# Where the spare PSUM bank is used inside an attention slot: next-batch work ahead of the query product

## The chip, the cores and the metric

The kernel runs on one core of one Trainium2 chip. The metric is the device time of one execution in microseconds (us), lower is better. One core has a matmul engine (TensorE, PE in the rows, its weight loads PEld), VectorE (DVE), ScalarE (ACT), GpSimd (POOL) and a queue for transfers (SyncE, SP). They run side by side, each strictly in its own program order, and meet only at semaphores.

## What is computed

A transformer-like stack on x of 4 batches x 512 tokens x 256 features, all in float32: a latent attention (16 heads, query rank 192, key/value rank 64), a feed-forward block with looked-up weights, a state-space scan block and the feed-forward block again, each behind a layer norm and added to x. The change touches only the attention, cut here to what matters:

```python
q_c  = rms_norm(x @ wq_down.T, q_norm_w)           # rank 192
kv_c = rms_norm(x @ wkv_down.T, kv_norm_w)         # rank 64
q_nope, q_pe = heads(q_c @ wq_up.T), rope(heads(q_c @ wq_rope.T))
k_nope, v = split(heads(kv_c @ wkv_up.T));  k_rope = rope(x @ wk_rope.T)
scores = (q_nope . k_nope + q_pe . k_rope) / sqrt(192), causal
out = softmax(scores) @ v;  return out @ wo.T
```

## The kernel before

**Precision.** Every float32 product is made of reduced-precision passes: an operand is split into a high part (ScalarE rounds it, `..._hi`) and a low part (VectorE subtracts, `..._lo`), and TensorE makes three products. So each operand that TensorE makes for itself goes PSUM bank, ScalarE copy, VectorE subtraction, in that order.

**Units and slots.** The attention of a batch is 16 units: 4 query tiles of 128 tokens x 4 groups of 4 heads. Tile i attends to i + 1 key tiles. The units run in a software pipeline written out by hand, one slot per unit: in slot s TensorE makes the query product of unit s (`q_up`, L1496 to L1500, bank 0), transposes the queries of unit s-2 (`q_transpose`, L1507, bank 1), makes the scores of units s-2 and s-3 (L629 to L631, banks 2 and 3), transposes the probabilities of unit s-4 (`p_transpose`, L1533, banks 4 and 5), multiplies them with the values for unit s-5 (L1547, L1550, bank 6) and projects unit s-6 (L1560, L1562, bank 7). Each engine has its own slot function (`pe_slot`, `act_slot`, `dve_slot`) that fixes the order of its instructions, and slots of one batch run on into the next. Below, slots are numbered through from 0 to 63 (batch times 16, plus the unit whose query product lies in it).

**VectorE's order.** Between two `qt_low` (L1153, the low part of the transposed queries) it does in this order: row maxima of the third head (L1129, `row_max`), `pt_low` of key tile 0 (L1181), row maxima of the fourth head, `out_low` (L1187), then the reciprocals, further splits, row maxima of the first two heads, the rotation of the next queries (`rope_q`, L1143 to L1148), and the next `qt_low`. The row maxima wait for the scores of the same head.

**The spare bank.** Bank 1 holds the transposed queries for a part of a slot. In the rest of it, in 27 of the slots, it makes one piece of the next batch's input: in slots 4 to 7 of a batch a down product (`down`, six matmuls of 320 columns on L629 to L631; ScalarE copies it, `down_copy`, L792), in slots 9 and 10 the transposed normalised input of the batch after (`pe_xt_part`, four transposes on L594; `act_xt_part` L599, `dve_xt_part` L603), in slots 12 to 14 the transposes to feature-major form (`to_features`, four transposes on L1481; `feature_high` L813, `feature_low` L1121). In the last batch only slots 14 and 15 have such a piece, the input transposes for the feed-forward block. The counts are 12 down products, 4 pieces of input transposes, 9 of features and 2 at the end. Called here a spare piece.

**What guards the bank.** Before a spare piece TensorE waits until `qt_low` of unit s-2 has read the bank (`pe.wait_ge(qt_lo_s, 1 + b * UNITS + s - 1)`). Before the next `q_transpose` it waits until the spare piece has been read (`dp_cp`, `xt_lo_s` or `at_lo`). Both are waits of an engine that works in order: everything written behind them waits too.

**GpSimd** builds the feed-forward weights all the while, one tensor operation after the other, to about 490 us.

Of the kernel before, what the change touches and what calls it, by code (L numbers as in the profile page):

```python
# [12 lines left out]
BATCH, SEQ, DIM = 4, 512, 256  # L13
# [94 lines left out]
def build(nc, x_in, wq_down, wq_up, wq_rope, q_norm_w, wkv_down, kv_norm_w, wkv_up, wk_rope, wo,  # L108
# [3 lines left out]
    with ctx:  # L112
# [658 lines left out]
        def _(act):  # L771
# [90 lines left out]
            def act_slot(s, b, nb):  # L862
                def do(step, n, *k):
                    step_of(b, nb, step, n, *k)

                do(normalise, s - 4, 2)
                do(normalise, s - 4, 3)
                do(exp, s - 3, 0)
                do(pt_high, s - 5, 3)
                do(qt_high, s - 2)  # L870
                do(exp, s - 3, 1)
                do(pt_high, s - 4, 0)
                do(out_high, s - 5)
                u, m = ahead(s, b, nb)
                if 5 <= u <= 8 and m < BATCH:
                    mean_squares(m, u - 5)
                do(exp, s - 3, 2)
                do(pt_high, s - 4, 1)
                do(exp, s - 3, 3)
                do(q_copy, s)  # L880
                u, m = ahead(s, b, nb)
                do(normalise, s - 3, 0)
                if m == BATCH:
                    if u in (14, 15):
                        act_xt_part(m, u - 14, bank[1])
                else:
                    if 4 <= u <= 7:
                        down_copy(m, u - 4)
                    if u in (9, 10) and m + 1 < BATCH:
                        act_xt_part(m + 1, u - 9, bank[1])  # L890
                    if 12 <= u <= 14:
                        feature_high(m, u - 12)
                do(normalise, s - 3, 1)
                do(pt_high, s - 4, 2)
                if u in (10, 11) and m < BATCH:
                    query_scale(m, u - 10)
# [168 lines left out]
        def _(dve):  # L1065
# [130 lines left out]
            def dve_slot(s, b, nb, early=(0, 0)):  # L1196
# [20 lines left out]
                if s >= 2:  # L1217
                    dve_tasks(dve, *early)
                do(recip, s - 3, 0)
                between(0)  # L1220
                do(pt_low, s - 4, 1)
                between(1)
# [2 lines left out]
                do(recip, s - 3, 1)  # L1225
                between(3)
                do(row_max, s - 2, 0)
                if m == BATCH:
                    if u in (14, 15):
                        dve_xt_part(m, u - 14, bank[1])  # L1230
                else:
                    if u in (9, 10) and m + 1 < BATCH:
                        dve_xt_part(m + 1, u - 9, bank[1])
                    if 12 <= u <= 14:
                        feature_low(m, u - 12)
                between(4)
                do(normalise, s - 3, 2)
                between(5)
# [224 lines left out]
        def _(pe):  # L1463
# [102 lines left out]
            def pe_slot(s, b, nb):  # L1566
                def do(step, n, *k):
                    step_of(b, nb, step, n, *k)

                do(values, s - 5, 0)  # L1570
                do(p_transpose, s - 5, 3)
                do(scores, s - 3, 1)
                do(values, s - 5, 1)
                u, m = ahead(s, b, nb)
                if m == BATCH:
                    if u in (15, 16):
                        pe.wait_ge(xt_lo_s, 2 * m + u - 14)
                else:
                    if 5 <= u <= 8:
                        pe.wait_ge(dp_cp, m * TB + u - 4)  # L1580
                    if u in (10, 11) and m + 1 < BATCH:
                        pe.wait_ge(xt_lo_s, 2 * (m + 1) + u - 9)
                    if 13 <= u <= 15:
                        pe.wait_ge(at_lo, 3 * m + u - 12)
                do(q_transpose, s - 2)
                do(p_transpose, s - 4, 0)
                do(values, s - 5, 2)
                do(scores, s - 3, 2)
                do(values, s - 5, 3)
                do(q_up, s)  # L1590
                do(scores, s - 3, 3)
                do(p_transpose, s - 4, 1)
                if m == BATCH:
                    if u in (14, 15):
                        pe.wait_ge(qt_lo_s, 1 + b * UNITS + s - 1)
                        pe_xt_part(m, u - 14, bank[1])
                else:
                    if 4 <= u <= 7 or u in (9, 10) or 12 <= u <= 14:

                        pe.wait_ge(qt_lo_s, 1 + b * UNITS + s - 1)  # L1600
                    if 4 <= u <= 7:
                        if u == 4:
                            wait_xt(pe, m)
                        down(m, u - 4)
                    if u in (9, 10) and m + 1 < BATCH:
                        pe_xt_part(m + 1, u - 9, bank[1])
                    if 12 <= u <= 14:
                        if u == 12:
                            pe.wait_ge(tok_q, TB * m)
                            pe.wait_ge(tok, token_count(m, 12))  # L1610
                        to_features(m, u - 12)
                do(project, s - 6)
                do(p_transpose, s - 4, 2)
                do(scores, s - 2, 0)
# [195 lines left out]
```

## Time and profile before

| | |
|---|---|
| time, median of 3 runs | 825.81 us (823.83 to 827.28) |
| time of the profiled execution | 823.76 us |
| its span, first to last instruction | 821.8 us |
| mean granted TensorE clock | 0.988 |
| busy in the span | PE 91%, DVE 82%, ACT 74%, POOL 56% |
| attention slots, from query product 0 to the end of slot 63 | about 40 to 533 us |

The table is read from the page of the profiled execution. The 2 us between its time and its span lie before the first and behind the last instruction. A line such as "start, length, engine, line, op, out<-in" of the timeline is one instruction; brackets at its end hold how long the engine was idle before it and who ended that.

### The profile page before, as it was taken

What the parts mean: (1) busy time and instruction counts of PE and PEld (TensorE: products, weight loads), DVE (VectorE), ACT (ScalarE), POOL (GpSimd) and SP (SyncE); (2) the same over time, 40 slices, a digit from 0 to 9 for tenths busy, and PEclk for the clock granted to TensorE, in tenths of its full rate; (3) what the DMA queues carried; (4) which work ended last, traced back from release to release, by engine and by line L of the source; (5) the groups of instructions that cost most, each with busy time, mean ns of one, the idle gap of its engine ahead of it and who ended that gap; (6) DMA issues with size and microseconds to landing.
All of it is one profiled execution on the core that took longest, in us unless ns stands there. A gap on an engine that the chain in (4) does not pass through costs nothing.

```text
span 821.8 us, 15155 instructions
## 1 busy us (share of the span) xinstructions
PE 752.0 (91%) x4556; PEld 646.4 (79%) x4556; DVE 674.5 (82%) x2204; ACT 609.7 (74%) x1512; POOL 461.5 (56%) x388
## 2 busy tenths in 40 slices
PE   3775999999999999999999899999998999999998
PEld 3665887878877887888888788877887798887887
DVE  3667899999899999899999999996765878777643
ACT  2454999988999988899988899986537565674222
POOL 1599999999999999999999999400000000000000
PEclk9897999999999999999999999999999999999999
DMA  9800000000000000000000100000000000000000
GB/s 243 279 1 0 2 1 2 1 1 1 2 2 1 2 1 1 2 2 1 2 1 2 39 2 1 2 1 0 2 1 0 1 1 1 1 1 27 27 26 26
DMA packets 15376, 14.52 MB, mean 18 GB/s; under 512 B 5792, under 2 KB 14432, under 8 KB 15040
## 3 DMA queue, kind: packets, MB, share of 16 engines
q1 hardware_dynamic: 13792, 11.41, 4.7%
q0 software_dynamic: 624, 2.12, 0.8%
q8 instruction: 37, 0.61, 0.3%
q14 instruction: 43, 0.35, 0.1%
q10 hardware_dynamic: 880, 0.04, 0.1%
HBM read 11.46 MB, written 2.10 MB: 17 GB/s over the span
## 4 chain that ended last, share of the span: by engine, by line
PE 52%; ACT 18%; DVE 16%; issue 13%; DMA 1%; DVEq 0%; ACTq 0%; SPq 0%
PE bank L629 11%; PE bank L631 10%; PE bank L630 10%; ACT prob L840 5%; PE bank L1533 5%; ACT prob L820 4%; DVE pt_lo L1181 2%; ACT pt_hi L849 2%; PE bank L1550 2%; PE bank L1547 2%; PE bank L1560 1%; PE bank L1562 1%; DVE bias_m L1129 1%; PE bank L594 1%; DVE qt_lo L1153 1%
## 5 line engine op out<-in xcount | busy, mean ns | idle before, releaser
L760 POOL TENSOR_SCALAR hot<-raw_gu,lut 128x352 f32<-128x352 int32 x120 | 177.9, 1482 | 12.2
L766 POOL TENSOR_TENSOR total<-total,hot 128x352 f32<-128x352 f32 (+1 forms) x168 | 158.7, 945 | 14.0
L820 ACT ACTIVATE prob<-bank,bias_m 128x128 f32<-128x128 f32 (+3 forms) x256 | 136.5, 533 | 21.0 <-DVE bias_m L1129 20.5
L1129 DVE CUSTOM_DVE_ANT_0 bank<-bank,mask 128x128 f32<-128x128 f32 (+3 forms) x256 | 125.4, 493 | 19.1 <-issue 17.7
L1181 DVE TENSOR_TENSOR pt_lo<-bank,pt_hi 128x512 fp32r<-128x512 f32 x160 | 108.9, 681 | 8.6 <-ACT pt_hi L849 8.3
L1533 PE MATMUL bank<-ident,prob 128*128 128x128 f32 x640 | 99.1, 277 | 17.5 <-ACT prob L840 11.2
L840 ACT ACTIVATE prob<-prob,rden 128x128 f32<-128x128 f32 (+3 forms) x224 | 110.4, 545 | 4.9 <-DVE rden L1164 4.3
L849 ACT CAST pt_hi<-bank 128x512 fp32r<-128x512 f32 x160 | 94.2, 590 | 11.5 <-PE bank L1550 6.9
L1533 PEld LDWEIGHTS bank<-ident,prob 128*128 128x128 f32 x640 | 72.4, 140 | 36.7 <-ACT prob L840 20.2
L629 PE MATMUL bank<-kt_hi,qt_hi 128*128 128x128 f32 (+3 forms) x256 | 87.4, 341 | 4.3 <-ACT prob L820 2.0
L760 POOL TENSOR_SCALAR hot<-raw_dn,lut 128x352 f32<-128x352 int32 (+1 forms) x60 | 87.6, 1461 | 6.1
L630 PE MATMUL bank<-kt_lo,qt_hi 128*128 128x128 f32 (+3 forms) x256 | 82.8, 324 | 0.0
L631 PE MATMUL bank<-kt_hi,qt_lo 128*128 128x128 f32 (+3 forms) x256 | 82.8, 323 | 0.0
L629 PE MATMUL bank<-xt_hi,gu_hi 128*128 128x512 f32 (+1 forms) x176 | 70.1, 399 | 1.6 <-DVE h_f L1305 1.6
L1547 PE MATMUL bank<-pt_hi,v_hl 128*128 128x512 f32 x160 | 68.1, 426 | 3.1 <-issue 2.4
L631 PE MATMUL bank<-xt_hi,gu_lo 128*128 128x512 f32 (+1 forms) x176 | 69.4, 394 | 0.0
L630 PE MATMUL bank<-xt_lo,gu_hi 128*128 128x512 f32 (+1 forms) x176 | 69.3, 394 | 0.0
L1560 PE MATMUL bank<-wo_a,o_a 128*128 128x256 f32 x256 | 67.9, 298 | 0.1
L933 ACT ACTIVATE silu<-bank 128x512 f32<-128x512 f32 x40 | 24.0, 601 | 57.4 <-PE bank L631 57.4
L1550 PE MATMUL bank<-pt_lo,v_hl 128*128 128x512 f32 x160 | 63.5, 397 | 0.3 <-DVE pt_lo L1181 0.2
L1562 PE MATMUL bank<-wo_b,o_b 128*128 128x256 f32 x256 | 63.7, 282 | 0.0
L629 PEld LDWEIGHTS bank<-kt_hi,qt_hi 128*128 128x128 f32 x256 | 48.6, 190 | 14.6 <-ACT prob L820 3.1
(208 smaller groups left out, 2091.9 us busy)
## 6 DMA issues: line engine op xcount, KB each, us to landing
x<-in_L_attn_a_x_dram SPq DMA_DIRECT2D x4, 512.0 KB, 7.7
wo_nat<-in_L_attn_a_wo_dram SPq DMA_DIRECT2D x1, 2048.0 KB, 12.2
out_dram<-x SPq DMA_DIRECT2D x16, 128.0 KB, 1.8
wqu<-in_L_attn_a_wq_up_dram SPq DMA_DIRECT2D x2, 768.0 KB, 7.7
wqr<-in_L_attn_a_wq_rope_dram SPq DMA_DIRECT2D x4, 192.0 KB, 7.5
raw_dn<-in_L_ffn_down_idx_dram POOLq DMA_DIRECT2D x1, 688.0 KB, 11.0
raw_gu<-in_L_ffn_gate_idx_dram POOLq DMA_DIRECT2D x1, 640.0 KB, 7.5
raw_gu<-in_L_ffn_up_idx_dram POOLq DMA_DIRECT2D x1, 640.0 KB, 8.5
```

The source lines that it names most:

```text
L629: nc.tensor.matmul(o, l_hi, r_hi, start=start and k == 0, stop=False)
L630: nc.tensor.matmul(o, l_hi, r_lo, start=False, stop=False)
L631: last = nc.tensor.matmul(o, l_lo, r_hi, start=False, stop=stop and k == n - 1)
L760: nc.gpsimd.tensor_scalar((hot if v else total)[:, 0:n], raw[:, c:c + n], float(v), lut[:, v:v + 1], ALU.is_equal, ALU.mult).then_inc(lut_ ...
L766: nc.gpsimd.tensor_tensor(dst, total[:, 0:n], hot[:, 0:n], ALU.add).then_inc(lut_sum, 1)
L820: nc.scalar.activation(prob[:, n % 2, h, 0:w], bank[2 + h % 2][:, 0:w], ACT.Exp, bias=bias_m[:, n % 2, h:h + 1], scale=-1.0, accum_out=den ...
L840: nc.scalar.activation(prob[:, n % 2, h, 0:w], prob[:, n % 2, h, 0:w], ACT.Copy, scale=rden[:, n % 2, h:h + 1]).then_inc(norm_a, 1)
L849: nc.scalar.copy(pt_hi[:, c % 2, :, :].rearrange("p h d -> p (h d)"), bank[4 + c % 2][:, :])\
L1129: nc.vector.tensor_tensor_reduce(out=bank[2 + h % 2][:, 0:w], in0=bank[2 + h % 2][:, 0:w], in1=mask[:, TB * P - w:TB * P], scale=1.0, scal ...
L1181: nc.vector.tensor_tensor(pt_lo[:, c % 2, :, :].rearrange("p h d -> p (h d)"), bank[4 + c % 2][:, :], pt_hi[:, c % 2, :, :].rearrange("p h ...
L1533: last = nc.tensor.transpose(bank[4 + c % 2][:, h * P:(h + 1) * P], prob[:, n % 2, h, j * P:(j + 1) * P], ident[:, :])
L1547: nc.tensor.matmul(bank[6][:, :], v, pt_hi[:, c % 2, :, :].rearrange("p h d -> p (h d)"), start=j == 0, stop=False)
```

## The change

In each of the three slot functions the spare piece moves forward, and nothing is added or removed. On TensorE it stood behind `p_transpose(s - 4, 1)` and now stands ahead of `q_up(s)`; its wait for `qt_lo_s` moves with it. On ScalarE the copy of the piece moves ahead of `pt_high(s - 4, 1)`. On VectorE the subtraction moves from behind `row_max(s - 2, 0)` to behind `recip(s - 3, 0)`. The wait ahead of `q_transpose` stays.

```diff
--- before.py
+++ after.py
@@ -875,11 +875,6 @@
                 if 5 <= u <= 8 and m < BATCH:
                     mean_squares(m, u - 5)
                 do(exp, s - 3, 2)
-                do(pt_high, s - 4, 1)
-                do(exp, s - 3, 3)
-                do(q_copy, s)
-                u, m = ahead(s, b, nb)
-                do(normalise, s - 3, 0)
                 if m == BATCH:
                     if u in (14, 15):
                         act_xt_part(m, u - 14, bank[1])
@@ -890,6 +885,11 @@
                         act_xt_part(m + 1, u - 9, bank[1])
                     if 12 <= u <= 14:
                         feature_high(m, u - 12)
+                do(pt_high, s - 4, 1)
+                do(exp, s - 3, 3)
+                do(q_copy, s)
+                u, m = ahead(s, b, nb)
+                do(normalise, s - 3, 0)
                 do(normalise, s - 3, 1)
                 do(pt_high, s - 4, 2)
                 if u in (10, 11) and m < BATCH:
@@ -1217,6 +1217,14 @@
                 if s >= 2:
                     dve_tasks(dve, *early)
                 do(recip, s - 3, 0)
+                if m == BATCH:
+                    if u in (14, 15):
+                        dve_xt_part(m, u - 14, bank[1])
+                else:
+                    if u in (9, 10) and m + 1 < BATCH:
+                        dve_xt_part(m + 1, u - 9, bank[1])
+                    if 12 <= u <= 14:
+                        feature_low(m, u - 12)
                 between(0)
                 do(pt_low, s - 4, 1)
                 between(1)
@@ -1225,14 +1233,6 @@
                 do(recip, s - 3, 1)
                 between(3)
                 do(row_max, s - 2, 0)
-                if m == BATCH:
-                    if u in (14, 15):
-                        dve_xt_part(m, u - 14, bank[1])
-                else:
-                    if u in (9, 10) and m + 1 < BATCH:
-                        dve_xt_part(m + 1, u - 9, bank[1])
-                    if 12 <= u <= 14:
-                        feature_low(m, u - 12)
                 between(4)
                 do(normalise, s - 3, 2)
                 between(5)
@@ -1587,9 +1587,6 @@
                 do(values, s - 5, 2)
                 do(scores, s - 3, 2)
                 do(values, s - 5, 3)
-                do(q_up, s)
-                do(scores, s - 3, 3)
-                do(p_transpose, s - 4, 1)
                 if m == BATCH:
                     if u in (14, 15):
                         pe.wait_ge(qt_lo_s, 1 + b * UNITS + s - 1)
@@ -1609,6 +1606,9 @@
                             pe.wait_ge(tok_q, TB * m)
                             pe.wait_ge(tok, token_count(m, 12))
                         to_features(m, u - 12)
+                do(q_up, s)
+                do(scores, s - 3, 3)
+                do(p_transpose, s - 4, 1)
                 do(project, s - 6)
                 do(p_transpose, s - 4, 2)
                 do(scores, s - 2, 0)
```

On TensorE, slot 25 (a piece of input transposes, `xn`), before: the query product is `wa_hi` to `wb_lo` into a bank, `kt_hi`/`qt_hi` are scores, `prob` is the probability transpose.

```order
L1496 MATMUL bank<-wa_hi,qa_hi 128x512 [waits q_rope,qa_cp]
L1497 MATMUL bank<-wa_lo,qa_hi 128x512
L1498 MATMUL bank<-wa_hi,qa_lo 128x512
L1499 MATMUL bank<-wb_hi,qb_hl 128x512
L1500 MATMUL bank<-wb_lo,qb_hl 128x512
L629 MATMUL bank<-kt_hi,qt_hi 128x256 [waits s_exp]
L630 MATMUL bank<-kt_lo,qt_hi 128x256
L631 MATMUL bank<-kt_hi,qt_lo 128x256
L1533 MATMUL bank<-ident,prob 128x128 [waits pt_lo_s]
L1533 MATMUL bank<-ident,prob 128x128 x3
L594 MATMUL bank<-ident,xn 128x128 [waits xt_lo_s,ln_norm,qt_lo_s]
L594 MATMUL bank<-ident,xn 128x128 x3
```

and now:

```order
L594 MATMUL bank<-ident,xn 128x128 [waits xt_lo_s,ln_norm,qt_lo_s]
L594 MATMUL bank<-ident,xn 128x128 x3
L1496 MATMUL bank<-wa_hi,qa_hi 128x512 [waits q_rope,qa_cp]
L1497 MATMUL bank<-wa_lo,qa_hi 128x512
L1498 MATMUL bank<-wa_hi,qa_lo 128x512
L1499 MATMUL bank<-wb_hi,qb_hl 128x512
L1500 MATMUL bank<-wb_lo,qb_hl 128x512
L629 MATMUL bank<-kt_hi,qt_hi 128x256 [waits s_exp]
L630 MATMUL bank<-kt_lo,qt_hi 128x256
L631 MATMUL bank<-kt_hi,qt_lo 128x256
L1533 MATMUL bank<-ident,prob 128x128 [waits pt_lo_s]
L1533 MATMUL bank<-ident,prob 128x128 x3
```

The two `xn` rows with their wait for `qt_lo_s` went from the end of this stretch to its head; the query product, the scores of the fourth head and the probability transpose stand behind that wait.

On VectorE, the same slot, before: `o_b` is `out_low`, `rden` a reciprocal, `pt_lo` the low part of the probabilities, `rms_...` and `x` small steps of other work, `ISA bank,bias_m` the row maxima, `xt_lo` the subtraction of the spare piece.

```order
L1187 TENSOR_TENSOR o_b<-bank,o_a 64x512 [waits o_hi_s]
L1164 RECIPROCAL rden<-den 128x2 [waits norm_a,s_exp]
L529 SCALAR_TENSOR_TENSOR rms_r<-rms_t,rms_r 128x8 [waits rms_ref]
L1181 TENSOR_TENSOR pt_lo<-bank,pt_hi 128x512 [waits pv_mm,pt_hi_s]
L636 TENSOR_TENSOR x<-bank,x 128x256 [waits y_mm]
L525 TENSOR_TENSOR rms_t<-rms_r 128x8 [waits rms_ref]
L1164 RECIPROCAL rden<-den 128x2 [waits norm_a,s_exp]
L527 SCALAR_TENSOR_TENSOR rms_t<-rms_t,rms_v 128x8 [waits rms_ref]
L512 MEMSET scratch 128x1 [waits s_exp,s_mm]
L1129 ISA bank,bias_m<-bank,mask 128x256
L1129 ISA bias_m 128x1
L603 TENSOR_TENSOR xt_lo<-bank,xt_hi 128x512 [waits xt_hi_s]
```

and now:

```order
L1187 TENSOR_TENSOR o_b<-bank,o_a 64x512 [waits o_hi_s]
L1164 RECIPROCAL rden<-den 128x2 [waits norm_a,s_exp]
L603 TENSOR_TENSOR xt_lo<-bank,xt_hi 128x512 [waits xt_hi_s]
L529 SCALAR_TENSOR_TENSOR rms_r<-rms_t,rms_r 128x8 [waits rms_ref]
L1181 TENSOR_TENSOR pt_lo<-bank,pt_hi 128x512 [waits pv_mm,pt_hi_s]
L636 TENSOR_TENSOR x<-bank,x 128x256 [waits y_mm]
L525 TENSOR_TENSOR rms_t<-rms_r 128x8 [waits rms_ref]
L1164 RECIPROCAL rden<-den 128x2 [waits norm_a,s_exp]
L527 SCALAR_TENSOR_TENSOR rms_t<-rms_t,rms_v 128x8 [waits rms_ref]
L512 MEMSET scratch 128x1 [waits s_exp,s_mm]
```

`xt_lo` moved up by nine rows, past one `pt_lo`, one reciprocal and the row maxima of one head. It is still behind `o_b`, and so behind the row maxima of the fourth head, which stand ahead of `o_b`.

On ScalarE, the same slot, before: `prob,den` is the exponential of one head, `pt_hi` the high part of the probabilities, `q_tok` the copy of the query product.

```order
L820 ACTIVATE prob,den<-bank,bias_m 128x256 [waits s_max]
L849 CAST pt_hi<-bank 128x512 [waits pv_mm,pt_mm]
L820 ACTIVATE prob,den<-bank,bias_m 128x256 [waits s_max]
L827 COPY q_tok<-bank 128x4x64 [waits qt_mm,qa_mm]
L840 ACTIVATE prob<-prob,rden 128x256 [waits recip_s]
L599 CAST xt_hi<-bank 128x512 [waits xt_mm]
L840 ACTIVATE prob<-prob,rden 128x256 [waits recip_s] x3
```

and now:

```order
L820 ACTIVATE prob,den<-bank,bias_m 128x256 [waits s_max]
L599 CAST xt_hi<-bank 128x512 [waits xt_mm]
L849 CAST pt_hi<-bank 128x512 [waits pv_mm,pt_mm]
L820 ACTIVATE prob,den<-bank,bias_m 128x256 [waits s_max]
L827 COPY q_tok<-bank 128x4x64 [waits qt_mm,qa_mm]
L840 ACTIVATE prob<-prob,rden 128x256 [waits recip_s] x4
```

`xt_hi` moved ahead of `pt_hi`, of the last exponential, of the query copy and of one normalisation (`prob<-prob,rden`).

## Rows read from the trace of the kernel before

**Rows 1.** The page's section 2, busy tenths of the span in 40 slices.

```profile
...
PE   3775999999999999999999899999998999999998
...
DVE  3667899999899999899999999996765878777643
...
```

**Rows 2.** Windows: slots with down products, with xn, with features, and the last two.

```profile
...
sum 72.34, PE 68.92 PEld 62.02 DVE 61.83 ACT 67.73 POOL 67.29; mean PE 22.97 PEld 20.67 DVE 20.61 ACT 22.58 POOL 22.43
...
sum 30.53, PE 28.00 PEld 23.92 DVE 30.14 ACT 29.45 POOL 28.40; mean PE 14.00 PEld 11.96 DVE 15.07 ACT 14.72 POOL 14.20
...
sum 74.44, PE 72.60 PEld 63.26 DVE 68.55 ACT 72.34 POOL 69.15; mean PE 24.20 PEld 21.09 DVE 22.85 ACT 24.11 POOL 23.05
...
519.49:536.95 17.46, 16.85 (x101) 13.95 (x101) 15.95 (x53) 15.87 (x39) 3.73 (x4) 1.00 0.01 1
...
```

**Rows 3.** Waits over the span: engine, line, releaser: us in total, times, longest.

```profile
...
PE bank L1507 <- DVE xt_lo L603: 2.2, 4, 1.2
```

**Rows 4.** Timeline of slot 21, a down product: start us, length us, instruction.

```profile
...
209.45 0.45 PE L1496 MATMUL bank<-wa_hi,qa_hi 128*128 128x512 f32 x1
209.47 0.69 DVE L1153 TENSOR_TENSOR qt_lo<-bank,qt_hi 128x512 fp32r<-128x512 f32 x1
...
210.31 0.69 DVE L1181 TENSOR_TENSOR pt_lo<-bank,pt_hi 128x512 fp32r<-128x512 f32 x1
...
210.93 0.36 PE L629 MATMUL bank<-down_hi,xt_hi 128*128 128x320 f32 x1
...
211.14 0.29 DVE L1129 CUSTOM_DVE_ANT_0 bank<-bank,mask 128x128 f32<-128x128 f32 x1
...
211.86 0.28 PE L1560 MATMUL bank<-wo_a,o_a 128*128 128x256 f32 x1
...
213.89 0.63 PE L1507 MATMUL bank<-ident,q_tok 128*128 128x128 f32 x4
...
214.65 0.60 ACT L832 CAST qt_hi<-bank 128x512 fp32r<-128x512 f32 x1
...
215.27 0.47 PE L1496 MATMUL bank<-wa_hi,qa_hi 128*128 128x512 f32 x1
...
```

**Rows 5.** Timeline of slot 25, a piece of input transposes.

```profile
...
234.65 0.40 PE L1496 MATMUL bank<-wa_hi,qa_hi 128*128 128x512 f32 x1
...
235.00 0.68 DVE L1153 TENSOR_TENSOR qt_lo<-bank,qt_hi 128x512 fp32r<-128x512 f32 x1
...
235.95 0.68 DVE L1181 TENSOR_TENSOR pt_lo<-bank,pt_hi 128x512 fp32r<-128x512 f32 x1
236.05 0.28 PE L631 MATMUL bank<-kt_hi,qt_lo 128*128 128x256 f32 x1
...
236.60 0.60 PE L594 MATMUL bank<-ident,xn 128*128 128x128 f32 x4
...
236.96 0.36 PE L1560 MATMUL bank<-wo_a,o_a 128*128 128x256 f32 x1
...
240.25 0.68 DVE L603 TENSOR_TENSOR xt_lo<-bank,xt_hi 128x512 fp32r<-128x512 f32 x1
...
240.98 0.66 PE L1507 MATMUL bank<-ident,q_tok 128*128 128x128 f32 x4 [1.18 <-DVE xt_lo L603]
...
```

**Rows 6.** Timeline of slot 29, a piece of feature transposes.

```profile
...
266.51 0.68 DVE L1153 TENSOR_TENSOR qt_lo<-bank,qt_hi 128x512 fp32r<-128x512 f32 x1
...
266.73 0.39 PE L1496 MATMUL bank<-wa_hi,qa_hi 128*128 128x512 f32 x1
...
267.60 0.68 DVE L1181 TENSOR_TENSOR pt_lo<-bank,pt_hi 128x512 fp32r<-128x512 f32 x1
...
268.63 0.56 DVE L1129 CUSTOM_DVE_ANT_0 bank<-bank,mask 128x384 f32<-128x384 f32 x1 [0.35 <-issue]
...
```

**Rows 7.** L1148 (79 to 530 us; busy, mean ns, idle), then min/median/max ns.

```profile
...
L1148 DVE TENSOR_TENSOR q_tok<-q_tok,q_rot 128x256 f32<-128x256 f32 x59 | 34.4, 582 | 2.0
...
L1148 DVE TENSOR_TENSOR q_tok<-q_tok,q_rot x64: 424/426/1216, 43.8 to 535.9; 128x256 f32<-128x256 f32 x64
...
```

## The prediction

> **What bounds the kernel now.** I read the page first: from slice 5 to slice 27 TensorE and VectorE both stand at eight or nine tenths [rows 1]. There are two full engines, so a wait on either can cost, and the share of busy time does not say which. I then took the windows of the slots that hold a spare piece. Each window runs from the end of one `qt_low` to the end of a later one, so that it holds whole VectorE periods: 80.74 to 104.17, 204.07 to 228.53 and 329.38 to 353.83 us for the 12 down products, 111.27 to 126.07 and 235.67 to 251.40 for the 4 `xn` pieces, 134.20 to 158.91, 259.53 to 284.25 and 382.18 to 407.19 for the 9 feature pieces, and 519.49 to 536.95 for the last 2 [rows 2]. A sum row gives the length of the windows and each engine's busy time in them. Subtracting, VectorE is idle 72.34 - 61.83 = 10.51, 30.53 - 30.14 = 0.39, 74.44 - 68.55 = 5.89 and 17.46 - 15.95 = 1.51 us, 18.30 us in all 27 periods. TensorE is idle 3.42 + 2.53 + 1.84 + 0.61 = 8.40 us. Neither has more than a few tenths of a microsecond to give in a slot, save VectorE in the down slots, with 0.88 us each.
>
> **What the move takes away.** The wait it can remove is the one ahead of `q_transpose`, where TensorE waits for `xt_lo` to be read out of bank 1. That is 2.2 us in 4 waits [rows 3], 1.18 us of it in slot 25: `xt_lo` runs from 240.25 to 240.93 and the transposes start at 240.98 [rows 5]. A semaphore therefore costs 0.05 us from end to start; I use that below. On VectorE `xt_lo` now stands nine rows earlier, so this wait should go. For down products and features no such wait shows, so nothing goes there.
>
> **What the move adds.** TensorE's wait for `qt_lo_s` stood 210.93 - 209.45 = 1.48 us behind the start of `q_up` in slot 21 [rows 4], where `qt_low` was long over. Now it stands where `q_up` started. Read both: in slot 21 TensorE started `q_up` at 209.45 and `qt_low` ended at 209.47 + 0.69 = 210.16 [rows 4]; in slot 25 it was 234.65 against 235.68 [rows 5]; in slot 29, 266.73 against 267.19 [rows 6]. TensorE would idle 0.71, 1.03 and 0.46 us, plus 0.05 each. Taken as the price per slot this gives 12 x 0.76 + 4 x 1.08 + (9 + 2) x 0.51 = 19.1 us, less 2.2 removed: 16.9 us. That is the ledger of TensorE.
>
> It is not the whole price, because of what is queued behind that wait: the spare piece itself, `q_up`, the scores of the fourth head, a probability transpose. VectorE's row maxima of the fourth head wait for those scores, and behind these row maxima stand all of `out_low`, the reciprocals, the rotation and the next `qt_low`. In place of running beside `qt_low`, the query product now lies between it and these row maxima. The ledger of VectorE, slot by slot:
> - Down, slot 21 [rows 4]. The piece takes 211.86 - 210.93 = 0.93 us. The row maxima start 211.14 - 209.45 = 1.69 us behind the start of `q_up`. New start: 210.16 + 0.05 + 0.93 + 1.69 = 212.83. VectorE is ready when `pt_low` ends, 210.31 + 0.69 = 211.00. It waits 1.83 us.
> - `xn`, slot 25 [rows 5]. The piece takes 236.96 - 236.60 = 0.36 us, and the scores end 236.33 - 234.65 = 1.68 us behind `q_up`. New start: 235.68 + 0.05 + 0.36 + 1.68 + 0.05 = 237.82, ready at 236.63: 1.19 us.
> - Features, slot 29 [rows 6]. Four transposes too, taken at 0.36 us; the row maxima start 268.63 - 266.73 = 1.90 us behind `q_up`. New start: 267.19 + 0.05 + 0.36 + 1.90 = 269.50, ready at 268.28: 1.22 us. The last 2 slots are taken as these.
>
> New waits: 12 x 1.83 + 4 x 1.19 + 11 x 1.22 = 22.0 + 4.8 + 13.4 = 40.2 us. VectorE does no more work than before, so its old idle time in the same periods, 18.3 us, is used up first. That leaves 21.9 us. The removed wait on `xt_lo` is not subtracted again: in these slots VectorE was busy in 30.14 of 30.53 us [rows 2], so the time TensorE gains there is time in which VectorE still has to work.
>
> Between the two ledgers, 16.9 and 21.9, I take VectorE's. TensorE's lag is itself made by the lateness of VectorE, and a period of VectorE cannot be shorter than its work and its waits.
>
> **Does the loss build up or wash out?** From below: if VectorE and ScalarE caught up behind the first wait, the lag would shrink to the bare chain. In slot 21 the query transposes take 0.63 us, the ScalarE copy 0.60 and `qt_low` 0.69, with two semaphores 2.02 us, while TensorE has 215.27 - 213.89 = 1.38 us of other work until `q_up` [rows 4]. So 0.64 us stays in each down slot, whatever the others do: 7.7 us for the 12. For the other slots I take no floor, and part of the 2.2 us is given back; about 7 us in all. From above: if VectorE's old idle time were only half usable, because it lies behind other waits, the sum would be 40.2 - 9.2 = 31 us. I keep 7 and 31 as the ends.
>
> **ScalarE.** Its copy of the piece moves into a stretch in which it now waits: the transposes for `pt_hi` and the scores for the last exponential come later by the piece and the wait. The copy costs nothing there, and as much less follows later. ScalarE was busy in 67.73 of 72.34 us in the down slots [rows 2], so it has little to give; its stream shifts with VectorE's, and I add nothing. If it were the one that ends last, the loss would lean to the upper end.
>
> **One outside influence on the lag.** L1148, the last step of the rotation, stands right ahead of `qt_low`. It takes 424 ns at best, 582 in the mean and 1216 at most [rows 7]; its operands are the same each time.
>
> The Trainium skill, SBUF — State Buffer, "Practical consequences", says that a VectorE instruction with two inputs in SBUF contends with a GpSimd instruction that reads SBUF, and that the later one blocks until the first is done. L1148 has two such inputs and GpSimd runs at that time, which would explain the spread. By that rule slots of another length meet GpSimd at other phases: with every L1148 of the 27 slots at 424 ns the sum would fall by 27 x 0.16 = 4.3 us, and with all of them held as long as the longest it would rise by 27 x 0.63 = 17 us. Which phase the changed kernel falls into no row tells.
>
> I leave the mean of 582 ns in the sum, as the rows have it.
>
> **The sum.** 823.76 us, the profiled execution, plus 21.9 gives 845.7. The median of the runs shown is 2.05 us above the profiled execution. I forecast 846 us, about half way towards the lower ledger with that offset added (823.8 + 2.0 + 20.2).
>
> **The rivals.**
> 1. Mostly absorbed, slower by 7 to 13 us, 831 to 837. After the first wait of each series the engines behind catch up, and only the bare chain of the down slots is left. For it: VectorE has 0.88 us idle per down slot. Against it: in the `xn` slots it has none.
> 2. It builds up, 856: ScalarE or the waits behind the fourth head's scores push the next `qt_low` further than TensorE's own delay, so the upper end of 31 us is met. For it: TensorE and ScalarE are both above nine tenths in the down slots [rows 2].
> 3. The other side, faster, about 821: the new wait hides in the idle time that TensorE has anyway. TensorE idles 8.40 us in these slots [rows 2]. If `qt_low` came so much earlier that the new wait fell under 0.3 us per slot, it would fit in there (27 x 0.3 = 8.1), and 2.2 us of `xt_lo` waits and a little more would be the net gain. This is decided by the lag between `q_up` and the end of `qt_low`; it must fall from 0.46 to 1.03 us to under 0.3. Against it stands the bare chain in the down slots, 0.64 us.
> 4. No change, 824 to 826: that waits cancel gains. It needs the same collapse of the lag, a little less of it.
>
> That the change does not take effect is excluded: the rows of all three engines are in another order.
>
> **How the numbers follow.** The forecast, 838 to 852, has a chance of 0.70; rival 1 has 0.15, rival 2 0.08, rival 3 0.03, rival 4 0.04. What this measurement can tell from no change is about 0.5%, 4.1 us. The first three are all slower by more than that: 0.93. Faster 0.03, same 0.04. The range reaches from 832, in rival 1, to 857, which takes in the upper end with its offset.
>
> **What will show it.** Right: in slots with a spare piece, the first instruction of the piece (L629 with `down_hi`, L594, L1481) has an idle time of 0.5 to 1.2 us ahead of it, ended by VectorE's `qt_lo`, 27 times; VectorE waits 1.2 to 1.8 us for the fourth head's row maxima; the waits of L1507 on `xt_lo` are gone; the 12 down periods last about 72.3 + 22.0 - 10.5 = 84 us in place of 72.3, and the feed-forward part is unchanged. Wrong: if the waits ahead of the pieces add up to under 8 us, `qt_low` does not lag as I read it; if they are there and the span has grown by much less, TensorE had slack that its busy share hides; if slots without a piece have grown, another engine carries the delay on.

## The result and the profile after

The changed kernel takes 865.62 us (857.65 to 867.28, 4 runs), against 826.54 us before on the same chip: ratio 1.047, 95% interval 1.044 to 1.051. The forecast was 846, slower by 20 us; it came out slower by 39. The direction and the place were right, the size was off by nearly a factor of two, and the time lies outside the stated range.

The page after, section 2: busy tenths per fortieth of the span, here 864.5 us, and the granted clock.

```profile
...
PE   4756778999888899888899999999998999999998
...
DVE  3676697899688889768889899898766778787643
...
PEclk9797999999899999999999999999999999999999
...
```

In the attention slots TensorE and VectorE have fallen together, in many slices from nine tenths [rows 1] to eight or less. Where the time went shows in the windows of the same 27 VectorE periods, found again by the ends of the same `qt_low`. First the three series of down products: stretch, length, busy time of PE, PEld, DVE, ACT, POOL, then the granted clock.

```profile
...
81.27:112.27 31.00, 25.55 (x152) 22.02 (x153) 20.33 (x90) 23.43 (x83) 28.88 (x24) 0.95 0.00 1
220.19:254.50 34.31, 29.36 (x168) 25.32 (x169) 22.46 (x94) 23.27 (x83) 31.91 (x27) 0.90 0.00 1
359.24:391.15 31.91, 26.42 (x169) 22.82 (x170) 21.48 (x90) 23.35 (x83) 29.67 (x25) 1.00 0.01 2
sum 97.22, PE 81.33 PEld 70.16 DVE 64.27 ACT 70.04 POOL 90.46; mean PE 27.11 PEld 23.39 DVE 21.42 ACT 23.35 POOL 30.15
```

Then the sums of the `xn` slots (2 windows) and of the feature slots (3 windows), and the window of the last two.

```profile
...
sum 38.29, PE 32.80 PEld 27.91 DVE 31.15 ACT 30.14 POOL 35.61; mean PE 16.40 PEld 13.96 DVE 15.57 ACT 15.07 POOL 17.81
...
sum 82.16, PE 76.43 PEld 66.11 DVE 68.08 ACT 72.56 POOL 76.31; mean PE 25.48 PEld 22.04 DVE 22.69 ACT 24.19 POOL 25.43
...
559.13:578.27 19.14, 18.35 (x106) 15.15 (x107) 16.04 (x53) 16.46 (x40) 0.00 (x0) 1.00 0.01 1
...
```

Against [rows 2] the periods grew by 24.9, 7.8, 7.7 and 1.7 us, 42.0 of the span's 42.7 us. So nearly the whole growth of the profiled execution lies in the periods with a piece. Who waited for whom on TensorE: the line that waited, the releaser, us in total, times, longest.

```profile
...
PE bank L629 <- DVE qt_lo L1153: 15.0, 12, 2.0
PE bank L1533 <- ACT prob L840: 13.5, 35, 0.9
PE bank L1481 <- DVE qt_lo L1153: 6.4, 9, 1.3
PE bank L594 <- DVE qt_lo L1153: 5.4, 6, 1.4
...
PE bank L1496 <- DVE qt_lo L1153: 1.7, 2, 1.1
...
```

The guard on `qt_low` costs TensorE 28.5 us in 29 waits. The wait for `xt_lo` [rows 3] is gone, as the change meant. Two of the 29 waits stand at L1496, the query product itself. In slots 41 and 42, in the third batch, the guard is executed though no piece follows: `u in (9, 10)` brings the guard, and only the piece asks for `m + 1 < BATCH`. I had counted pieces, not guards.

One down slot, 38, at full clock: start, length, engine, line, operation; brackets give the idle time before and its end.

```profile
...
372.61 0.63 PE L1507 MATMUL bank<-ident,q_tok 128*128 128x128 f32 x4
...
373.47 0.57 ACT L832 CAST qt_hi<-bank 128x512 fp32r<-128x512 f32 x1
...
373.89 1.03 DVE L1148 TENSOR_TENSOR q_tok<-q_tok,q_rot 128x256 f32<-128x256 f32 x1
...
374.84 0.68 DVE L1153 TENSOR_TENSOR qt_lo<-bank,qt_hi 128x512 fp32r<-128x512 f32 x1
...
375.57 0.41 PE L629 MATMUL bank<-down_hi,xt_hi 128*128 128x320 f32 x1 [1.36 <-DVE qt_lo L1153]
...
376.56 0.39 PE L1496 MATMUL bank<-wa_hi,qa_hi 128*128 128x512 f32 x1
...
378.21 0.29 DVE L1129 CUSTOM_DVE_ANT_0 bank<-bank,mask 128x128 f32<-128x128 f32 x1 [1.86 <-issue]
...
378.60 0.37 ACT L820 ACTIVATE prob<-bank,bias_m 128x128 f32<-128x128 f32 x1 [1.38 <-DVE bias_m L1129]
...
```

Read it downwards: query transposes, then the copy, over at 373.47 + 0.57 = 374.04 us; `qt_low` starts 0.80 us later, held back by a long L1148; TensorE is released 0.05 us behind its end; the piece, the query product, and at 378.21 the row maxima of the fourth head, for which VectorE waited 1.86 us (the forecast had 1.83). ScalarE's exponential then waits 1.38 us for those. In slot 21 before, TensorE and VectorE did not wait there [rows 4], and neither did ScalarE.

This slot is no exception in what held `qt_low` back. VectorE's row for it over the whole span: count, busy us, mean ns, idle us before it.

```profile
...
L1153 DVE TENSOR_TENSOR qt_lo<-bank,qt_hi 128x512 fp32r<-128x512 f32 x64 | 43.7, 683 | 0.6 <-ACT qt_hi L832 0.2
...
```

VectorE was idle only 0.6 us in total ahead of all 64, 0.2 us of it for the copy. In the timeline, the 27 `qt_low` that a piece waits for start on average 0.65 us behind the end of their copy (0.57 before the change); in 25 of them the copy had been over for 0.27 us or more, and what ended last was VectorE's own work ahead of it: the last step of the rotation (L1148) in 19 of the 27, small steps for the next batch in most others.

### The profile page after: what moved, and what is told of

Same layout as the page of the kernel before. It is cut to its first block, busy times and chain, and to the rows that moved or that the text cites. A ratio compares the mean times of both kernels' runs of the same rounds, so it can differ in the third digit from the quotient of the medians.

```text
span 864.5 us, 15154 instructions
## 1 busy us (share of the span) xinstructions
PE 764.8 (88%) x4556; PEld 654.0 (76%) x4556; DVE 675.6 (78%) x2204; ACT 611.8 (71%) x1512; POOL 460.7 (53%) x388
## 4 chain that ended last, share of the span: by engine, by line
PE 50%; DVE 21%; issue 18%; ACT 9%; DMA 1%; DVEq 0%; ACTq 0%; SPq 0%
PE bank L629 10%; PE bank L631 10%; PE bank L630 10%; PE bank L1533 4%; DVE pt_lo L1181 3%; ACT prob L840 3%; ACT prob L820 2%; DVE qt_lo L1153 2%; DVE bias_m L1129 2%; DVE o_b L1187 2%; PE bank L1550 2%; PE bank L1547 2%; ACT pt_hi L849 2%; PE bank L594 2%; PE bank L1560 1%
## 5 line engine op out<-in xcount | busy, mean ns | idle before, releaser
L1129 DVE CUSTOM_DVE_ANT_0 bank<-bank,mask 128x128 f32<-128x128 f32 (+3 forms) x256 | 125.7, 495 | 60.3 <-issue 57.2
L766 POOL TENSOR_TENSOR total<-total,hot 128x352 f32<-128x352 f32 (+1 forms) x168 | 158.2, 942 | 14.0
L1533 PE MATMUL bank<-ident,prob 128*128 128x128 f32 x640 | 99.3, 278 | 19.1 <-ACT prob L840 13.5
L840 ACT ACTIVATE prob<-prob,rden 128x128 f32<-128x128 f32 (+3 forms) x224 | 107.1, 541 | 5.8 <-DVE rden L1164 5.1
```

The source lines that it names most:

```text
L766: nc.gpsimd.tensor_tensor(dst, total[:, 0:n], hot[:, 0:n], ALU.add).then_inc(lut_sum, 1)
L840: nc.scalar.activation(prob[:, n % 2, h, 0:w], prob[:, n % 2, h, 0:w], ACT.Copy, scale=rden[:, n % 2, h:h + 1]).then_inc(norm_a, 1)
L1129: nc.vector.tensor_tensor_reduce(out=bank[2 + h % 2][:, 0:w], in0=bank[2 + h % 2][:, 0:w], in1=mask[:, TB * P - w:TB * P], scale=1.0, scal ...
L1533: last = nc.tensor.transpose(bank[4 + c % 2][:, h * P:(h + 1) * P], prob[:, n % 2, h, j * P:(j + 1) * P], ident[:, :])
```

## The experiments

Each time below stands beside the kernel before on the same chip, 825.3 to 826.3 us. Ratios are to it, with the 95% interval. The edits are shortened: `(guard, piece)` stands for the wait on `qt_lo_s` and the spare piece behind it.

**Which pieces?** `down_early`: only the down products moved, on TensorE and ScalarE. `others_early`: all but them moved.

```diff
+if down_slot:  (guard, down)      # others_early: if not down_slot
 do(q_up, s)
 do(scores, s - 3, 3)
 do(p_transpose, s - 4, 1)
+if not down_slot:  (guard, piece)
```

> Only the 12 down products stand ahead of the query product (TensorE) and ahead of the probability split (ScalarE); the xn, feature and last pieces stay where they were before. Theory A (each moved piece puts the wait for qt_low ahead of the query product, and the row maxima of the fourth head wait for it; the prices of the kinds of piece simply add): the down periods grew by 23.9 us in the trace of the changed kernel, so about 848 to 852 us here, clock below 0.985. Rival B (the pieces spoil each other, the delay of one series is carried into the next by ScalarE): clearly less than its share, under 840 us.

> The 15 other pieces (xn, features, the last two) stand early on all three engines, the down products as before; the guard on qt_low stands early in every slot that had it. Theory A: 6.2 + 8.0 + 1.4 us of their periods plus 1.8 us of two slots that have the guard and no piece, 17 us, so about 842 to 845 us. The early guard ahead of the query product also stands in the two slots of batch 3 without a piece. Rival B: under its share, near 835 us, with the missing rest appearing only when both moves are made together.

Measured: 847.79 us, 1.025 (1.021 to 1.030), and 843.56 us, 1.022 (1.019 to 1.024). The added times over the kernel before, some 21 and 18 us (2.53% and 2.16% of 826), add up to 39, with some 4 us of uncertainty, and both moves together gave 39.1. Theory A stands: each moved piece has its own price, and B, that one series spoils the next, is refuted to within that.

**The guard or the piece?** `guard_only` is the kernel before with the guard alone ahead of `q_up`. `behind_q_up` has piece and guard between `q_up` and the scores of the fourth head, so late that the guard hardly waits. `guard_all` is `guard_only` with the guard in all 60 slots from slot 4 on.

```diff
 # guard_only                                   # behind_q_up
+if slot_has_guard:                              do(q_up, s)
+    pe.wait_ge(qt_lo_s, 1 + b*UNITS + s - 1)   +(guard, piece)
 do(q_up, s)                                     do(scores, s - 3, 3)
```

> The kernel before, with only the guard added: in the slots that have one, TensorE also waits for qt_low ahead of the query product; the pieces themselves and ScalarE and VectorE stay where they were. Theory A (VectorE's wait for the fourth head's row maxima sets the price, and of its old idle time only that at the same place is used up): 0.58 x 12 + 0.83 x 4 + 0.33 x 11 + 1.8 us, about 16 us, and some 3 us for the clock: 840 to 846 us. Rival F (only the wait of TensorE counts and the piece ahead of the query product costs nothing): the whole loss appears here, 860 us or more.

> ScalarE and VectorE as in the changed kernel, on TensorE the piece and its guard directly behind the query product and ahead of the scores of the fourth head. qt_low is over by then (the lag is under the 1.2 us of a query product in all but a few slots), so what is left is that the scores, and the row maxima behind them, come later by the piece. Theory A: 0.93 x 12 + 0.36 x 15, less 2.2 us of waits for xt_lo, about 14 us and no more falls of the clock: 836 to 842 us. Rival F: about 824 to 828 us, since no wait of TensorE is added.

> The kernel before with the guard on qt_low ahead of the query product in all 60 slots from slot 4 on, in place of the 29 of guard_only: the suspected cost doubled. Theory A (each guard costs about 0.83 us, since qt_low lags by that in every slot): 826 + 60 x 0.83 = 876 us, 870 to 885. Rival K (the cost is one of changing from one rhythm to another, and washes out where the wait is everywhere): under 860 us.

Measured: `guard_only` 850.46 us, 1.030 (1.026 to 1.034); `behind_q_up` 834.37 us, 1.010 (1.008 to 1.011); `guard_all` 884.24 us (2 runs), 1.071 (1.069 to 1.073). TensorE's waits in the first and in the last, and the one left in `behind_q_up` on a down product:

```profile
...
PE bank L1496 <- DVE qt_lo L1153: 26.6, 29, 1.7
...
```

```profile
...
PE bank L1496 <- DVE qt_lo L1153: 53.8, 60, 2.0
...
```

```profile
...
PE bank L629 <- DVE qt_lo L1153: 1.1, 1, 1.1
...
```

The guard alone costs 24.2 us for 26.6 us of waiting, and 60 guards cost 58.9 for 53.8. In these two kernels what TensorE waits there is lost nearly one for one, and K, that the cost washes out where the wait is everywhere, is refuted. My theory A had 14 to 20 us for `guard_only`, by VectorE's ledger, and was short again; rival F, that the guard is everything, was too high. The piece ahead of the scores costs 8.1 us by itself, under the 10 to 16 I expected; F, which had it at nothing, fails here as well. Together 32.3 of 39.1 us. That the two prices simply add is assumed, not shown.

**Whose lateness makes the lag?** Four kernels cut one VectorE instruction to 32 of its 512 columns, `out_low` (not between the transposes and the guard) or `qt_low` (between them), in the changed kernel and in the one before.

```diff
+if b or n > 1:      # changed_light, before_light: out_low; changed_qt_light, before_qt_light: qt_low
+    nc.vector.tensor_tensor(<32 columns>, ..., ALU.subtract).then_inc(<the same semaphore>, 1)
+    return
```

> The changed kernel with out_low (L1187) cut from 512 to 32 columns in all but the first two units: it leaves out most of the low part of the attention output, so only its time is read. out_low stands directly behind the row maxima of the fourth head on VectorE and takes some 0.6 us per slot. Theory H (the ring wait for qt_low, query product, row maxima, VectorE's stream, next qt_low sets the period of a slot with a piece): the time falls by about 0.5 us x 29 slots more than in the kernel before with the same cut: by 15 us or more, to 846 to 852 us. Rival J (the ring goes over the query transposes and ScalarE's copy): it falls by no more than the kernel before does.

> The kernel before with the same cut of out_low, the control of changed_light; most of the low part of the attention output is left out. VectorE is the fullest in the xn slots and in the slots of the fourth query tile, so some of the 0.6 us x 64 is seen there: 812 to 822 us under either theory. What counts is the difference to the changed kernel's fall.

> The changed kernel with qt_low (L1153) cut from 512 to 32 columns in all but the first two units: it leaves out most of the low part of the transposed queries, so only its time is read. VectorE loses the same 0.6 us per slot as in changed_light, but here the cut lies between the query transposes and the guard. Theory J (the price is TensorE's wait for the chain query transposes, ScalarE's copy, qt_low, whatever else VectorE has to do): the waits ahead of the pieces fall from 29 us by about 0.5 us each, and the time by at least 14 us, to 851 us or less, clearly more than the 6 us that the cut of out_low gave. Theory H (VectorE's whole stream sets the period): the same 6 us as there, 859 us.

> The kernel before with the same cut of qt_low, the control. Nothing waits for qt_low itself here before the scores 2 us later, so what is seen is VectorE's relief alone: about as with the cut of out_low, 815 us, 810 to 820, under either theory.

| cut | before, us and ratio | changed, us and ratio | fall of before | fall of changed |
|---|---|---|---|---|
| none | 826.54, 1 | 865.62, 1.0471 | | |
| `out_low` | 814.85, 0.9869 | 859.34, 1.0415 | 0.0131, 10.8 us | 0.0056, 4.6 us |
| `qt_low` | 822.54, 0.9954 | 848.75, 1.0261 | 0.0046, 3.8 us | 0.0210, 17.3 us |

The falls are differences of the ratios, times 826 us; each ratio has an interval of 0.002 to 0.004 to either side, so the falls of the changed kernel are good to some 4 us. Either cut takes 0.50 us off each of 62 instructions (684 to 184 ns, 683 to 181). The same relief of VectorE is worth 12.7 us more in the changed kernel when it is taken from `qt_low` itself, and less than half as much in the kernel before, where I had expected 810 to 820 us and was wrong. The waits of the down products and of the feature pieces in `changed_light`, then in `changed_qt_light`. The inserted lines move L1481 to L1485, and in the second L1153 to L1154:

```profile
...
PE bank L629 <- DVE qt_lo L1153: 15.8, 12, 2.0
...
PE bank L1485 <- DVE qt_lo L1153: 4.7, 9, 0.9
...
```

```profile
...
PE bank L629 <- DVE qt_lo L1154: 6.1, 10, 1.5
...
PE bank L1485 <- DVE qt_lo L1154: 2.5, 5, 0.8
...
```

H's forecast failed and J's came true: `out_low`, though it stands in VectorE's stream to the next `qt_low`, gives little, and the 29 waits stay as they are (28.4 us in `changed_light`, 28.5 without the cut); `qt_low` itself gives 17.3 us, 0.6 per guard. That the length of `qt_low` is part of the price is thus shown. J as a whole is not: it names the query transposes and ScalarE's copy as what comes before, and in the changed kernel the copy was over 0.65 us ahead of `qt_low`. Part of what `out_low` gave up turned into waiting further on in VectorE's order; its idle time ahead of the row maxima, 60.3 us in the changed kernel, is here

```profile
...
L1129 DVE CUSTOM_DVE_ANT_0 bank<-bank,mask 128x128 f32<-128x128 f32 (+3 forms) x256 | 125.7, 495 | 69.5 <-issue 64.6
...
```

No run cut the row maxima or the rotation, which stand between.

**Bringing `qt_low` forward.** In the slots ahead of a piece, `qt_low` moves ahead of the rotation.

```diff
+if next_slot_has_piece: do(qt_low, s - 1)
 do(rope_q, s)
 ...
-do(qt_low, s - 1)
+if not next_slot_has_piece: do(qt_low, s - 1)
```

> The changed kernel, but in the slots ahead of a piece VectorE makes qt_low ahead of the rotation of the next queries, so that the rotation (1.3 us) fills VectorE's wait for the fourth head's row maxima and qt_low is over sooner. Theory A: the row maxima's wait falls from 2.2 to about 0.9 us in a down slot, and what is left is the bare chain transposes, copy, qt_low: 838 to 846 us. Rival G (ScalarE's or TensorE's own stream carries the loss, VectorE's order is second to it): 856 us or more.

Measured 865.71 us, 1.045 (1.039 to 1.050): nothing gained. My expectation of 838 to 846 failed, and the time is in the range of rival G. A wait of VectorE, then three of TensorE (the query product is L1502 here, the feature transposes L1487):

```profile
...
DVE qt_lo L1153 <- ACT qt_hi L832: 20.5, 27, 1.2
...
```

```profile
...
PE bank L629 <- DVE qt_lo L1153: 7.4, 10, 2.2
PE bank L1487 <- DVE cd L1110: 7.4, 3, 2.8
PE bank L1502 <- DVE q_rot L1146: 5.7, 17, 1.4
...
```

The guards did come free sooner: TensorE waits for `qt_low` 9.7 us in all (7.4 at down products, 2.3 at `xn` pieces) in place of 28.5. But `qt_low` now stands waiting for the copy for 20.5 us, with the rotation behind it. The next query product waits until the rotation has read its bank, 5.7 us in place of 0.5, and three feature pieces wait 7.4 us for L1110, the last step of the next batch's key rotation, which stood ahead of `qt_low` and now stands behind it. So 18.8 us less waiting at the guard bought no time: the one-for-one rule of `guard_only` holds for a guard moved along TensorE's order, not for every way of shortening its wait. The profiled execution is also the slowest of the four, at a mean clock of 0.970, so a part of the missing gain may be clock; that was not separated.

**The granted clock.** `filled` puts six matmuls of no use ahead of the guard in the down and `xn` slots, `filled_more` four more in slot 12 of a batch.

```diff
+for _ in range(6):
+    nc.tensor.matmul(bank[<free>][:, 0:DOWN], down_hi[:, 0, 0:P], down_hi[:, 0, :], start=True, stop=True)
 (guard, piece)
```

> The changed kernel with six extra matmuls of 320 columns (0.93 us at full clock), of no use and into a probability bank that is free there, ahead of the wait for qt_low in the slots of down products and xn pieces, so that TensorE does not stand idle. Theory C (part of the loss is the granted clock, which fell in slots 10, 20 and 21 because TensorE idled): clock back to 0.986 or more, and the time falls by 5 to 10 us in spite of more work, to 856 to 861 us. Rival D (the clock is no part of the loss, the wait chain alone is): 866 us or more, since 18 x 0.93 us are added and some stand on the path.

> As filled (six idle matmuls ahead of the guard in the down and xn slots), and four more in the first feature slot of a batch, where the granted clock still fell in the trace of filled. Theory C: the clock no longer falls behind slot 4, 0.986 or more in the profiled run, and the time is 856 to 861 us, at or a little under filled. Rival D: the clock falls as often and the time stays at 861 us or rises.

Measured 861.45 us, 1.043 (1.041 to 1.045), and 863.09 us, 1.044 (1.040 to 1.047). The same stretch around slots 20 to 22 in `filled`, at full clock:

```profile
...
200.00:256.00 56.00, 51.55 (x344) 45.00 (x343) 45.16 (x171) 45.43 (x146) 52.00 (x44) 1.00 0.00 1
...
```

D, that 18 x 0.93 us of extra work must cost, is not what happened: the matmuls mostly fill waits, and the guards wait 12.6 us in place of 28.5. With C the sign agrees, though the clock reached 0.982 to 0.984 and not the 0.986 it asked for. The intervals touch that of the changed kernel (1.044 to 1.051), and `filled_more` did not go on falling: the size is not settled by these. Two readings give its order. The down series of 220 us took 34.31 us at a clock of 0.90, the equal one of 359 us 31.91 at 1.00, and before they took 24.46 and 24.45: 2.4 us for that series. In it, behind a wait of TensorE of 1.96 us, the matmuls of the query product at 221.39 us took 0.63 us each, against 0.39 in slot 38. Of the two `xn` windows, the one at a clock of 0.91 grew by 5.1 us and the one at 1.00 by 2.7, another 2.3 us; but the first down series, at 0.95, grew by 7.6 us, hardly more than the 7.5 of the one at 1.00. And the changed kernel ran once in 857.65 us with a mean clock of 0.984, three times in 864.98 to 867.28 with 0.976 to 0.978: 7 to 10 us between runs of one program. My estimate from these is about 5 to 9 us of the 39.

**The two guards without a piece.** `no_idle_guard` asks for `m + 1 < BATCH` in the guard too.

> The changed kernel without the guard in the two slots of batch 3 (slots 41 and 42) that have a guard and no piece. Theory A: their TensorE periods fall back from 7.24 and 7.85 us to about 6.4 and 6.9, and the time by 1 to 2 us, which one look cannot tell from the changed kernel; the trace shows it. Otherwise the periods stay and something else holds them.

One run: 860.61 us. TensorE's periods of slots 41 and 42, from one group of query transposes to the next, fell from 7.24 and 7.85 to 6.59 and 7.43 us, 1.1 us together. The rest of the difference to the median is within what single runs of this kernel spread.

**Is there a gain in it at all?** `behind_scores`: all pieces behind the scores of the fourth head, ahead of the probability transpose. `others_behind`: the same, with the down products where they were.

```diff
 do(q_up, s)
 do(scores, s - 3, 3)
+(guard, piece)               # others_behind: if not down_slot
 do(p_transpose, s - 4, 1)
+if down_slot: (guard, down)  # others_behind only
```

> ScalarE and VectorE as in the changed kernel, but on TensorE the piece and its guard stand behind the query product and the scores of the fourth head, only ahead of the probability transpose. Theory A: qt_low is done by then and the row maxima wait for nothing new, so the loss is gone and the 2.2 us of waits for xt_lo too: 820 to 826 us. Rival E (a good part of the loss comes from the earlier places on ScalarE and VectorE): 835 us or more.

> Down products as in the kernel before on TensorE and ScalarE; the xn, feature and last pieces behind the scores of the fourth head on TensorE, early on ScalarE and VectorE as in the changed kernel. The waits for xt_lo should go and no wait for qt_low is left. Theory A: 822 to 826 us, at best 2 us under the kernel before. Rival E (early places on ScalarE and VectorE cost by themselves): 828 us or more.

Measured: 825.22 us, 0.9995 (0.997 to 1.002), and 824.70 us, 0.998 (0.996 to 0.9999). E is refuted: with TensorE's piece behind the scores, the earlier places on ScalarE and VectorE cost nothing. The waits for `xt_lo` are gone in both. `others_behind` is 0.2% under the kernel before, with its interval ending at 0.9999; among this many variants that is no proof of a gain.

## Why the prediction was wrong in size

- **The place and the sign: right.** 27 pieces wait for `qt_low`, L1507 no longer waits for `xt_lo`, VectorE waits at the fourth head's row maxima, and outside the 27 periods the span grew by only 0.7 us. The down periods last 97.2 us in place of the 84 forecast.
- **The failed step, "its old idle time in the same periods, 18.3 us, is used up first".** VectorE's idle time in the 27 periods is now 97.22 - 64.27 + 38.29 - 31.15 + 82.16 - 68.08 + 19.14 - 16.04 = 57.3 us, 39.0 more than 18.3. By place, from the timelines: ahead of the fourth head's row maxima it went from 1.9 to 48.1 us, 46.2 more where the forecast had 40.2; ahead of the first head's, from 8.0 to 0.4; everywhere else, from 8.4 to 8.9. So 7.6 of the 18.3 us were used up, and the rest recurred behind the new wait. VectorE's busy time in these periods also grew, by 3.1 us. Together this is the growth of 42 us, against 21.9.
- **A sum that would have agreed by chance.** Without that subtraction the sum would have read 823.8 + 2.0 + 40.2 = 866.0 us, the time measured. It would have been right in part by luck: a new wait forecast 6 us too short against 7.6 us that were indeed used up.
- **The choice of the ledger.** I chose VectorE's over TensorE's, because "TensorE's lag is itself made by the lateness of VectorE". The rows bear the sentence out as far as 0.65 us of each lag: `qt_low` comes that much behind its copy. But lateness further back hardly counts, as the cut of `out_low` shows (4.6 us), and `qt_low_first` took most of the 0.65 us away and saved nothing. The sentence did not justify the subtraction.
- **TensorE's ledger, taken from one slot per kind, was mis-sized.** I had 19.1 us from slots 21, 25 and 29, two of which have the shortest lags of their kinds or nearly so. The same lag read at all 27 pieces of the kernel before comes to 27.0 us, and with the two guards that I missed to 29.5. The 29 guards in `guard_only` wait 26.6 us, 0.92 each. Its waits for `xt_lo` fell by 1.6 us, from 2.2 to 0.6, which leaves 25.0, close to the 24.2 measured for the guard alone.
- **Two guards were missed**, 1.1 to 1.7 us.
- **The piece ahead of the scores** costs 8.1 us more; I had it only inside VectorE's ledger.
- **The clock** was in no case of mine. 24.2 + 8.1 leaves 6.8 us, which is of the size of the estimate for the clock. What else is in it stays open: the guards wait 1.9 us longer in the changed kernel than in `guard_only`, and the end of the waits for `xt_lo` is counted in both prices.
- **The rivals.** The bare chain of 0.64 us per down slot was a sound lower bound. "It builds up", 856, pointed the right way and not far enough. Of its two mechanisms, the waits behind the fourth head's scores did grow beyond my sum; ScalarE's own part was isolated by no run. The absorbing rival had the reasoning of the ledger in it and was wrong with it.
- **L1148.** Its mean over the span was 571 ns before and 547 after, and ahead of the 27 `qt_low` that count 590 and 569, so the phase against GpSimd did not carry the loss. In the slot shown above it took 1.03 us from 373.89, and GpSimd's L766, which reads two tensors from SBUF, ran from 373.71 to 374.64. That row agrees with the rule of the Trainium skill (SBUF — State Buffer, "Practical consequences") on a VectorE instruction with two inputs in SBUF beside a GpSimd instruction that reads SBUF.

## What to carry to other kernels

A guard that costs nothing where it stands is priced by how long before that point its condition came true. When it is moved up by more than that slack, the engine waits for the difference in every repetition, and here that was lost nearly one for one (26.6 us of waiting, 24.2 us of time). Sum the lag over every repetition, not over one sample of each kind, and count the guards as executed, not the work behind them.

Idle time of another engine may be subtracted only where the delay can soak it up: here 7.6 of 18.3 us, all ahead of one group of instructions, and the rest came again behind the new wait. To find out what an instruction on that engine is worth, shorten it alone, in both versions, and compare with one further back; read in the trace what ended last ahead of it before naming the chain.

The transfer of a shared buffer forward is worth at most the wait that its return ends (here 2.2 us), so look for the latest place that still ends it.

## What was not expected of the hardware

The granted TensorE clock fell again in mid-kernel. After, it was 0.83 from 221.40 to 240.70 us, where TensorE had waits of 1.15 and 1.32 us ahead of pieces, and one of 1.96 us that ended just before the stretch, and was busy in 15.65 of 19.30 us; no single wait of it there reached 2.0 us. In the down series at 359 us TensorE was busy in 26.42 of 31.91 us, about the same share, and the clock stayed at 1.00. What made the difference between the two stays open. Of four runs of the same program, the one with a mean clock 0.006 to 0.008 higher took 7 to 10 us less.
